# Latent attention: probabilities transposed three slots behind their scores

## The reference, cut to what matters

```python
q_hk = (hidden_q @ Wq.T).reshape(Bv, Sv, H, K)
q_big = jnp.einsum('bshk,hkq->bshq', q_hk, w_kc_q)
q_big = _apply_rope(q_big, sin_q[None, :, None, :], cos_q[None, :, None, :])
kv_r = _apply_rope(kv_c, sin_k[None], cos_k[None])
q_r = jnp.einsum('bshq,hqr->bhsr', q_big, W_qr)
k_r = jnp.einsum('bld,hdr->bhlr', kv_r, W_kr)
scores = jnp.einsum('bhsr,bhlr->bhsl', q_r, k_r)
attn = jax.nn.softmax(scores, axis=-1)
ctx_c = jnp.einsum('bhsl,bld->bhsd', attn, kv_r)
ctx_lat = jnp.einsum('bhsd,hkd->bhsk', ctx_c, w_kc_kv)
ctx = ctx_lat.transpose(0, 2, 1, 3).reshape(Bv, Sv, H * K)
return ctx @ Wo.T
```

## Time and profile before

| | us |
|---|---|
| median of 3 runs | 2024.52 |
| the three runs | 2023.42, 2024.52, 2028.41 |
| the profiled execution's own time | 2027.26 |
| its span, first to last instruction | 2025.5 |
| PE busy | 1837.5 (91%) |
| DVE busy | 1398.9 (69%) |
| ACT busy | 974.6 (48%) |
| POOL busy | 680.3 (34%) |

### The profile page before, as it was taken

The page is one execution under the profiler, slowest core; times in us unless marked ns, Lnnn a source line. Parts: engine busy times, 40 slices in busy tenths (PEclk is TensorE's granted clock), DMA queues, the critical chain, the costliest instruction groups (busy, mean ns, idle before and its releaser), DMA issues. The chain is left out here.

```text
span 2025.5 us, 31266 instructions
## 1 busy us (share of the span) xinstructions
PE 1837.5 (91%) x11244; PEld 1445.7 (71%) x11258; DVE 1398.9 (69%) x2821; ACT 974.6 (48%) x2042; POOL 680.3 (34%) x628
## 2 busy tenths in 40 slices
PE   4899999999999899998987997999968899999996
PEld 4677887777877687777763544666538789999996
DVE  5776677777678677888767884677836437666664
ACT  3444444543544344443444654655433236666663
POOL 4332122332623212332101131232322564566553
PEclk9999999999999999999997998999979999999999
DMA  5022201220311321222125111000041457777783
GB/s 203 17 85 82 79 28 62 85 89 1 118 39 36 128 81 37 73 93 97 37 60 212 47 38 42 1 2 1 1 162 38 138 98 231 227 246 239 231 243 74
DMA packets 52397, 192.38 MB, mean 95 GB/s; under 512 B 7678, under 2 KB 11902, under 8 KB 41494
## 3 DMA queue, kind: packets, MB, share of 16 engines
q1 hardware_dynamic: 40550, 167.01, 23.5%
q0 software_dynamic: 11408, 23.37, 6.3%
q10 hardware_dynamic: 288, 0.00, 0.0%
HBM read 156.99 MB, written 33.36 MB: 94 GB/s over the span
## 5 line engine op out<-in xcount | busy, mean ns | idle before, releaser
L363 POOL TENSOR_TENSOR la_q_roped<-la_q_roped 128x400 f32<-128x400 f32 x128 | 139.5, 1111 | 682.5 <-DVE la_q_roped L819 682.5
L722 ACT ACTIVATE la_probs<-banks,la_minus_max 100x361 f32<-100x361 f32 x256 | 144.7, 565 | 195.1 <-DVE la_minus_max L909 195.1
L819 DVE TENSOR_TENSOR la_q_roped<-banks,la_rope_q 128x400 f32<-128x400 f32 x384 | 197.0, 565 | 26.7 <-PE banks L490 16.2
L2072 DVE TENSOR_TENSOR ex_weights_low<-ex_raw_weights,ex_weights_high 128x2048 fp32r<-128x2048 f32 x60 | 137.6, 2293 | 53.4 <-ACT ex_weights_high L1967 50.4
L527 PEld LDWEIGHTS banks<-identity,la_probs 100*121 100x121 f32 x768 | 113.0, 184 | 71.1 <-DVE la_probs L916 45.7
L916 DVE TENSOR_SCALAR la_probs<-la_probs,la_rsum 100x361 f32<-100x361 f32 x256 | 152.2, 595 | 9.1
L538 PE MATMUL banks<-la_probs_t,la_kv_rows 121*128 121x200 f32 x768 | 151.4, 333 | 0.0
L2339 POOL TENSOR_TENSOR ex_g_low<-ex_g,ex_g_high 128x256 fp32r<-128x256 f32 (+1 forms) x104 | 86.7, 950 | 179.1 <-ACT ex_g_high L2011 178.6
L909 DVE TENSOR_REDUCE la_minus_max<-banks 100x1 f32<-100x361 f32 x256 | 134.9, 527 | 16.1 <-PE banks L518 9.4
L527 PE MATMUL banks<-identity,la_probs 100*121 100x100 f32 x768 | 126.1, 273 | 21.8 <-DVE la_probs L916 18.2
L1967 ACT CAST ex_weights_high<-ex_raw_weights 128x2048 fp32r<-128x2048 f32 x60 | 114.2, 1903 | 41.8 <-PE banks L2420 35.1
(11 more groups left out here) (335 smaller groups left out, 5279.3 us busy)
## 6 DMA issues: line engine op xcount, KB each, us to landing
ex_raw_weights<-w_exp SPq DMA_DIRECT2D x60, 1024.0 KB
la_weights<-w_pack SPq DMA_DIRECT2D x15, 1856.0 KB, 7.9
la_kv_turned<-w_ffn SPq DMA_DIRECT2D x30, 384.0 KB
la_rope_k<-w_ffn SPq DMA_DIRECT2D x30, 384.0 KB
qf_sign_weights<-ffn_signs SPq DMA_DIRECT2D x3, 2048.0 KB, 10.2
ffn_signs<-la_ffn_signs SPq DMA_DIRECT2D x30, 192.0 KB, 2.1
residual<-x SPq DMA_DIRECT2D x2, 2048.0 KB, 14.4
out<-ex_block_out POOLq DMA_DIRECT2D x13, 256.0 KB, 5.0
```

Of the source, the lines that this page charges most:

```text
L363: pool.tensor_tensor(roped[:, h, 0, c, :], roped[:, h, 0, c, :], roped[:, h, 1, 1 - c, :], ALU.add).then_inc(b_add, 1)
L722: act.activation(prob[:, s % 4, 0:L], ps[0:S, s % 2, 0:L], ACT.Exp, bias=nmax[:, s % 4:s % 4 + 1], accum_out=sums[:, s % 4:s % 4 + 1]).the ...
L819: dve.tensor_tensor(roped[:, h, v, c, :].rearrange("p (b s) -> p b s", b=GB), ps[:, B_BANKS[k % 2], 0:NT].rearrange("p (b s) -> p b s", b=GB),
L2072: dve.tensor_tensor(wl[:, m, :], raw[:, m, :], wh[:, m, :].bitcast(F32), ALU.subtract).then_inc(w_low[m], 1)
```

## The change: what it does

```diff
@@ -225,7 +225,7 @@
         UNITS = 2 * (HT // NT)
         ITEMS = 2 * HB
         SCALE_AT, SIGN_AT = (ITEMS, ITEMS + 2), (ITEMS + 2, ITEMS + 4)
-        MIX, OUT = 5, 8
+        TURN, MIX, OUT = 3, 6, 9
         SLOTS = OUT + ITEMS - 1
         AHEAD = (SLOTS - 6, SLOTS - 2)
 
@@ -611,8 +611,8 @@
                         if ends_half(n) and s == TURN_AT[0]:
                             pe.wait_ge(q_sum, 1)
                             pe.matmul(ps[:, C_BANKS[0], 0:3], ones[:], wtot[:], start=True, stop=True).then_inc(q_total, 1)
-                        if 2 <= s < ITEMS + 2:
-                            turn_probs(n, s - 2)
+                        if TURN <= s < ITEMS + TURN:
+                            turn_probs(n, s - TURN)
                         if s in AHEAD and n + 1 < RUNS:
                             first_units(n + 1, AHEAD.index(s))
 
@@ -731,8 +731,8 @@
                                 act.wait_ge(o_psum, n * HB + b - 1)
                             act.copy(ch[:, b % 2, :, :].rearrange("p h s -> p (h s)"),
                                      ps[:, V_BANK, 0:2 * S]).then_inc(v_high, 1)
-                        if 2 <= s < ITEMS + 2:
-                            j = s - 2
+                        if TURN <= s < ITEMS + TURN:
+                            j = s - TURN
                             b = j // 2
                             act.wait_ge(t_psum, n * ITEMS + j + 1)
                             if b >= 2:
```

## The result

The changed kernel takes 2038.13 us, median of six runs (2034.32 to 2042.22); the kernel before took 2024.83 beside it (six runs, 2023.28 to 2028.41). The ratio is 1.0066, 95% interval 1.0049 to 1.0083: 13.3 us slower. The forecast was 2036, slower.

The account below looks back on a forecast made before the run. PE was busy 938 of 997 us; only its 18.2 us of waits for DVE's products could be won. Passes +10.0, pass 7 +2.6, pass 10 -1.1 gave +11.5 us: about 2036 by the median, range 2021 to 2045.

Parts of the forecast that it names:

- Turn 0's wait buys nothing: Slots 2 and 3: removing the 0.79 us wait wins nothing, since the narrow still starts 0.08 after the ropes' end.
- The second wait goes: Slot 3, 12 passes: the 0.40 us wait ahead of turn 1 disappears; scores(5) starts 0.47 earlier.
- Maximum(4) 0.66 earlier, so the absorb 0.66 earlier; a wait of 1.36 there: Slots 4 to 5: `wout_low` moves behind maximum(4); PE waits 1.36 us for the rank copy, where it waited 0.36.
- Slot 7, "so I count nothing": Turn 4 waits some 0.3 us for item 3's copy, as large as slot 6's present wait; counted as 0.
- Pass 7, +2.6: Slots 8 to 15: ACT and DVE set the pace, 4 pairs costing 0.32 + 0.32 each; bounds 0 and 4.
- Pass 10, -1.1: Head of pass 10: DVE's late chunks end earlier relative to PE, so 1.1 us of the stall is won.
- The clock: Pass 10: about 1.6 us lost to a lowered clock; the stall stays long enough, so no change was counted.
- Twelve passes of one kind and four of the other: 12 passes with the second wait lose 0.60 us each; passes 1, 2, 4 and 15, without it, 0.71 each.
- the waits vanish and none comes back: Rival, decided at slot 5's absorb: rank copy ready when scores(5) ends, 9.1 us won over 12 passes; 2017; chance 0.14.
- ACT falls behind: Rival: turns 4 to 6 wait for the bank, or maximum is no earlier; 1.2 per pass, 2045; chance 0.08.
- Half of it: Rival: item 4's exponential comes still earlier, loss per pass 0.3 or less, about +5; 2029 or so; chance 0.18.
- the clock stays up in pass 10: Rival: as forecast, less 1.6 us because the stall in pass 10 becomes shorter; 2034.5; chance 0.10.

Follow-up runs that it names:

- e11: Changed kernel with POOL's split held back, plus the transpose of item 0 and its copy back in slot 2: 2019.85 us, ratio 0.9968.
- e3: Changed kernel with DVE's low part of the output weights back in slots 3 and 4: 2058.06 us, ratio 1.0126.
- e1: Mix, out and the output weights' low part one slot later than in the kernel before, transposes still two slots behind: 2031.44 us, ratio 1.002.

## Why the prediction was right, step by step

The direction and the mechanism at the absorb were right, and +11.5 was summed where +13.3 was measured; that the total is so near owes something to terms that miss on opposite sides. By its own steps:

- *Turn 0's wait buys nothing.* Right. The narrow starts 0.09 behind the ropes' end as before, and bringing turn 0 back with its wait made the kernel 4.4 us faster (e11).
- *The second wait goes.* Right as to the wait. It won its 0.4, and the absorb gave it back.
- *Maximum(4) 0.66 earlier, so the absorb 0.66 earlier; a wait of 1.36 there.* The step was right to the hundredth: scores(2) to absorb takes 8.71 us for 9.37. The wait is right too. Reckoned by starts, as the 1.36 was, it is 849.84 less 847.94 and the 0.55 of scores(5), 1.35; the 1.19 of the list begins only where the last matmul's record ends. For the same reason the 0.36 of before, which the prediction sets beside its 1.36, is 0.53 by starts. The low part put back cost just this 0.66 (e3).
- *Slot 7, "so I count nothing".* The sum had 0.60 a pass, and measured is 0.85. The prediction was right that the wait is there before as well, in slot 6, though the list of waits does not show it; by starts it grew by 0.15, alike in passes 5 to 14. The other 0.10 comes behind slot 7: from scores(8) to the next pass's scores(2) the owed mix and turn were to take 1.26 and 1.35 was measured, and no row found carries the rest. The two make some 3 to 4 us over the passes, on one side, and pass 7 stands on the other, so that the total came out nearer than its terms. That much is luck.
- *Pass 7, +2.6.* Mis-sized, and the most of all terms. The step from pass 7 to 8 adds 1.7, 0.9 over the others, and the fall of the clock at its end, 1.6, is more than all of that; without it the pass would be some 0.75 shorter than the others' change, under the lower bound of 0. The direction of the term shows: the turns' waits in the slots behind the head rose from 2.07 to 2.69. That is 0.6, not 2.6, and it is outweighed by the widen's wait of 1.28 for the last split, which is gone with the 24th slot. The prediction had no term for that.
- *Pass 10, -1.1.* Right: the wait at the widen fell from 4.9 to 3.0, and the two steps from 8 to 10 add 1.4 us less than two others.
- *The clock.* "Count nothing" held for pass 10, where the granted clock was still 0.78. It did not hold elsewhere: in this execution it fell behind the absorb of pass 3 (some 1.3 us) and at the end of pass 7 (1.6), where it had stayed up before. Whether it does so in every execution one profile cannot tell.
- *The other three parts only start later.* They do: the last absorb is 14.9 us later in the profiled execution, the span 15.0 longer.

Twelve passes of one kind and four of the other was nearly right too, but the kinds are not fixed: pass 4, which had no second wait before, became one in which DVE is late (absorb's wait 1.71), because POOL's split (L390 at 321.90) now met two products of its head, of 2.12 and 1.88 us, of which the first had taken 0.41 before. Pass 0 went the other way (absorb's wait 0.40).

Of the rivals, *the waits vanish and none comes back* would have been true with two more edits; with them (rank copy first, POOL's split late) the lag of three is still no faster than the lag of two. So the place named as deciding, the absorb, is a first gate only: with it open the wait went on to the copy out of the one bank. *ACT falls behind* was seen in that form, and not in the change itself, where the new wait in slot 7 is 0.24 only. *Half of it* and *the clock stays up in pass 10* did not come. The first of these was also added up wrong: 16 x 0.3 and 1.5 are 6.3, not 5, and 2031.

What stays open: by the medians the mix accounts for 3.4 of the 13.3 us and by the pass in the trace for 0.5 of 0.85. The gain in pass 10 and the falls of the clock in passes 3 and 7, which the profile of e1 does not have, go some way between the two; how much of the 13.3 the falls are was not measured. And by what the clock's falls come in one pass and not in the next was not settled.

## What to carry to other kernels

A wait is worth removing only if what stands behind it could start earlier: look at what the next instruction on that engine is pinned by, before the wait is costed. Work that PE does while a chain of other engines runs covers that chain: if it is moved away, the wait comes back at the chain's end. Small waits are to be compared by the starts of the instructions on both sides: the list of waits had the one of 0.24 in slot 7 and not the one of before in slot 6, and between them lay only 0.15. And a pass of another kind is to be walked through to its last slot. Here the lever was neither the lag nor the order on PE but what made DVE late, a side job on POOL that could run some ten microseconds later in the pass (L390 from 7.1 us ahead of the absorb to 3.3 behind it, on the kernel before), with a gain of 8.5 us.

## What the runs showed of the hardware

- One POOL instruction on a wide tile stretches a DVE instruction to more than four times its time: the product takes 0.41 us alone, 1.88 beside POOL's 2.35 us, ending just after it (847.97, POOL at 847.76). With POOL's split moved it was 0.41. The Trainium skill ("SBUF — State Buffer", section "Who interferes with whom") has the two engines share a pair of ports: when a DVE instruction runs in a mode that uses both of its port pairs, as a `tensor_scalar` like this product can, the one that comes first holds the shared pair for its whole instruction while the other is blocked. The trace agrees.
- The granted clock can fall behind short waits. With `wout_low` put back it fell in eight heads of passes, where four waits of some 0.2 to 1.9 us (2.4 in one) stand close together, and not in others with the same waits (pass 6 against pass 7 above). Each fall cost about 1.5 us. In the kernel before it fell, from pass 1 to the end of the stage, only at the stall of 4.9 us in pass 10. And behind one and the same wait of 1.25 us at the end of pass 7 it fell in six of the fourteen profiled executions and stayed up in the others.
- It may make the time less certain too: the four runs of the kernel with eight falls in its profiled execution took 2045.85 to 2060.27 us, at a mean clock of 0.968 and 0.965, while the ten runs of the one with the mix alone lay within 6.2 us. With four runs this is a hint only; 25 runs of the kernel before lay within 13.2.
